# Second attention over the context replanned, self-attention masks split between two engines

## The reference, cut to what matters

```python
# cross: 16 heads of 64; query = layernorm(x), keys and values from the context
q = (einsum('btd,dhk->bthk', query, Wq) + bq) / 8
k = einsum('bsd,dhk->bshk', key, Wk) + bk
v = einsum('bsd,dhk->bshk', value, Wv) + bv
probs = softmax(einsum('bshk,bthk->bhts', k, q))
out = einsum('bthk,hkd->btd', einsum('bhts,bshk->bthk', probs, v), Wo) + bo

# self: 8 heads of 64, 5 experts, 2 chosen
wv = topk_mask(x @ Ws, 2) * sigmoid(x @ Ws)
v = einsum('bthe,btek->bhtk', wv, einsum('btd,edk->btek', x, Wv))
attn = softmax(q k^T / 8) v
out = einsum('bthe,bthk,ekd->btd', topk_mask(x @ Wd, 2), attn, Wo)
```

## Time and profile before

| | |
|---|---|
| median of 3 runs | 2669.01 us (2666.1 to 2669.58) |
| the profiled execution: time, span | 2665.16 us, 2663.4 us |
| TensorE busy, weight load | 2396.2 us (90%), 1526.1 us (57%) |
| VectorE, ScalarE, POOL busy | 1830.3 (69%), 1203.5 (45%), 857.8 us (32%) |
| mean granted clock of TensorE | 0.942 |
| first instruction of cross, of self (POOL) | 1081.82, 2160.16 us |

### The profile page before, as it was taken

How to read it: one execution, slowest core, us unless ns; L and a number is a source line. 1 busy time by engine, 2 the same in 40 slices (tenths; PEclk the granted TensorE clock), 3 DMA queues, 4 the chain that set the end, 5 groups by cost and what they waited for, 6 DMA issues and landing times. The chain is left out here.

```text
span 2663.4 us, 36143 instructions
## 1 busy us (share of the span) xinstructions
PE 2396.2 (90%) x13376; PEld 1526.1 (57%) x13376; DVE 1830.3 (69%) x3190; ACT 1203.5 (45%) x2092; POOL 857.8 (32%) x469
## 2 busy tenths in 40 slices
PE   5999999999999689799999999999999958889896
PEld 3555655655655477555565556555665545556564
DVE  6998898798788577456655665565556537867673
ACT  4555455445454200244444444444444413756485
POOL 3421221222222000175545554555455711101010
PEclk9999999999999789799999999999999977888887
DMA  3000000000000111400000000000000010000000
GB/s 110 15 1 24 17 1 25 17 1 1 17 1 1 48 40 39 117 13 1 1 24 16 1 1 25 16 1 1 1 17 1 1 59 9 1 1 24 16 1 24
DMA packets 62632, 48.62 MB, mean 18 GB/s; under 512 B 12226, under 2 KB 61954, under 8 KB 62466
## 3 DMA queue, kind: packets, MB, share of 16 engines
q1 hardware_dynamic: 62468, 46.40, 5.7%
HBM read 38.01 MB, written 8.39 MB: 17 GB/s over the span
## 5 line engine op out<-in xcount | busy, mean ns | idle before, releaser
L436 POOL TENSOR_TENSOR cross_acc_pool<-cross_acc_pool,cross_probs 128x1024 f32<-128x1024 f32 x192 | 464.4, 2419 | 163.7 <-ACT cross_probs L517 149.6
L634 DVE TENSOR_REDUCE cross_part<-cross_ring 128x1 f32<-128x512 f32 x512 | 322.7, 684 | 99.0 <-PE cross_ring L771 98.9
L422 POOL TENSOR_TENSOR latent_KR<-latent_rot 128x256 f32<-128x256 f32 x128 | 176.1, 1375 | 606.7 <-DVE latent_rot L628 606.7
L517 ACT ACTIVATE cross_probs<-cross_scores 128x1024 f32<-128x1024 f32 x256 | 256.5, 1026 | 169.4 <-PE cross_scores L803 165.8
L517 ACT ACTIVATE latent_probs<-latent_scores 128x1024 f32<-128x1024 f32 x256 | 247.7, 1020 | 86.6 <-PE latent_scores L799 86.6
L663 DVE TENSOR_TENSOR latent_acc_dve<-latent_acc_dve,latent_probs 128x1024 f32<-128x1024 f32 x192 | 258.1, 1344 | 10.0
L819 PE MATMUL cross_outT<-cross_probs,cross_VN 128*64 128x512 f32 x1024 | 250.3, 610 | 0.0
L819 PE MATMUL latent_outT<-latent_probs,latent_VN 128*64 128x512 f32 x1024 | 247.9, 605 | 0.7 <-DVE latent_probs L649 0.7
L771 PE MATMUL cross_ring<-cross_KH,cross_QH 64*128 64x512 f32 x512 | 153.3, 475 | 40.8 <-DVE cross_newt L670 23.4
L649 DVE TENSOR_SCALAR latent_probs<-latent_probs 128x1024 f32<-128x1024 f32 x256 | 167.7, 695 | 9.4 <-ACT latent_probs L517 9.3
L436 POOL TENSOR_TENSOR cross_acc_pool<-cross_probs 128x1024 f32<-128x1024 f32 x32 | 76.3, 2384 | 299.4 <-PE cross_ring L831 262.9
(11 more groups left out here) (290 smaller groups left out, 5639.0 us busy)
## 6 DMA issues: line engine op xcount, KB each, us to landing
latent_C<-in_ctx_dram SPq DMA_DIRECT2D x4, 1024.0 KB, 6.5
cross_C<-in_ctx_dram SPq DMA_DIRECT2D x4, 1024.0 KB, 6.5
latent_XN<-in_x_dram SPq DMA_DIRECT2D x4, 512.0 KB, 3.9
latent_WRAW<-in_L_xattn_Wkv_dram SPq DMA_DIRECT2D x16, 128.0 KB, 2.4
latent_X<-in_x_dram SPq DMA_DIRECT2D x4, 512.0 KB, 3.8
x_after<-latent_X SPq DMA_DIRECT2D x4, 512.0 KB, 2.9
experts_raw<-in_L_ffn_expert_w_dram SPq DMA_DIRECT2D x1, 2048.0 KB
experts_XN<-x_after SPq DMA_DIRECT2D x4, 512.0 KB, 4.0
```

The costliest lines, as they stand in the source:

```text
L422: nc.gpsimd.tensor_tensor(KR[:, 2 * t:2 * t + 2, :], rot1s[n % 2][:, :, :], rot2s[n % 2][:, :, :], ALU.add)\
L436: nc.gpsimd.tensor_tensor(acc_pool[:, :, :], first[:, :, :], probs[g % PROBS][:, :, :], ALU.add)\
L517: nc.scalar.activation(probs[g % PROBS][:, :, :], scores[g % 2][:, :, :], ACT.Exp, scale=SCALE)\
L634: nc.vector.reduce_max(part[:, qt, h, i:i + 1], bank[:, :], AX.X).then_inc(taken, 1)
```

## The change

Cross: K(s+2, 1) moves to d = 3 of step s, one step earlier than before, and K(s+2, 0) to d = 1, q(s+2) to d = 2; V stands at d = 0 and 2. `between` is empty: the maxima stand two before and two after the scores of each part. At d = 0 `behind` comes ahead of `front`. The turns of the next batch are spread one or two to a part, and K, shift and q follow them. The first output tile moves from d = 1 to d = 2. `norm` is ScalarE's correction (2 - newt) and two POOL products. The shift's operands are rounded, in cross and in self. In self, masks 1 and 3 become one VectorE product of 128x640 each.

```diff
-            for t, d in enumerate((1, 2, 3, 3)):
+            for t, d in enumerate((1, 2, 3, 3) if latent else (2, 2, 3, 3)):
                 put(late, s, d, ("out", b - 1, t))
...
         if more:
-            put(tail, s, 0, ("K", s + 1, 1))
             maxima = [("max", s + 1, qt, i, h) for i in range(KT // 4) for qt in range(QT) for h in range(2)]
-            for d, place in ((0, between), (0, mid), (1, front), (1, between), (1, mid), (2, front), (2, mid), (3, front)):
-                put(place, s, d, *maxima[:2])
-                maxima = maxima[2:]
+            for d in range(parts):
+                put(front, s, d, *maxima[4 * d:4 * d + 2])
+                put(mid, s, d, *maxima[4 * d + 2:4 * d + 4])
+        group, half = divmod(s + 2, 2)
+        if group < steps // 2:
+            if group * 2 // NP == b:
+                for i in range(2):
+                    put(tail, s, 2 * i, ("V", group, 2 * half + i))
+            elif half == 1:
+                for t in range(parts):
+                    put(tail, s, t, ("V", group, t))
+        entering = p == NP - 2 and b + 1 < B
+        if entering:
+            n = b + 1
+            put(tail, s, 0, turn(n, "c", 0, 0), ("sum", s - 1))
+            put(tail, s, 1, ("norm", s - 1), turn(n, "c", 1, 0), turn(n, "c", 0, 1))
+            put(tail, s, 2, ("K", s + 2, 0), turn(n, "c", 1, 1), turn(n, "x", 0))
+            put(tail, s, 3, turn(n, "x", 1), ("K", s + 2, 1), ("shift", s + 1), ("q", s + 2))
+            continue
         if s > 0:
             put(tail, s, 0, ("sum", s - 1))
             put(tail, s, 1, ("norm", s - 1))
...
-        elif s + 2 < steps:
-            put(tail, s, 2, ("K", s + 2, 0))
+        if s + 2 < steps:
+            put(tail, s, 1, ("K", s + 2, 0))
+            put(tail, s, 2, ("q", s + 2))
+            put(tail, s, 3, ("K", s + 2, 1))
         if more:
             put(tail, s, 3, ("shift", s + 1))
...
-            plan += front[n] + behind + scores + mid[n]
+            plan += behind + front[n] + scores + mid[n]
...
-            negtop = sb("negtop", [P, QT, 2, DH])
+            negtop = sb("negtop", [P, QT, 2, DH], f32r)
...
+                elif kind == "norm" and not latent:
+                    s = item[1]
+                    b, p = divmod(s, NP)
+                    pool.wait_ge(corrected, s + 1)
+                    nc.gpsimd.tensor_tensor(newt[:, :], newt[:, :], guess[:, :], ALU.mult).then_inc(newt_steps, 1)
+                    pool.wait_ge(newt_steps, s + 1)
+                    pool.wait_ge(evacuated, s + 1)
+                    nc.gpsimd.tensor_tensor(OT[:, p, :], OT[:, p, :], newt[:, :], ALU.mult).then_inc(normed, 1)
...
+                elif kind == "norm" and not latent:
+                    s = item[1]
+                    act.wait_ge(*freed(("sum", s)))
+                    nc.scalar.activation(newt[:, :], newt[:, :], ACT.Copy, scale=-1.0, bias=2.0).then_inc(corrected, 1)
...
                         last = nc.tensor.matmul(bank[:, qt * P:(qt + 1) * P], negtop[:, qt, :, :].rearrange("p h d -> p (h d)"),
-                                                ident[:, :], start=True, stop=True)
+                                                identr[:, :], start=True, stop=True)
...
-                elif kind == "mask":
+                elif kind == "mask" and item[2] in (0, 2):
...
+                elif kind == "mask" and item[2] in (1, 3):
+                    _, s, t = item
+                    if t == 1:
+                        dve.wait_ge(*freed(("back", s)))
+                        dve.wait_ge(scales_made, s + 1)
+                        if s >= 2:
+                            dve.wait_ge(mix_steps, mix_before[s - 1])
+                    nc.vector.tensor_tensor(masked[s % 2][:, t, :, :, :],
+                                            natural[s % 2][:, t, :, :].unsqueeze(1).broadcast_to([P, EXPERTS, 2, DH]),
+                                            scaled[s % 2][:, t, :, :].rearrange("p h e -> p e h").unsqueeze(3)
+                                            .broadcast_to([P, EXPERTS, 2, DH]), ALU.mult).then_inc(rows_gated, 1)
...
-                    dve.wait_ge(rows_masked, QT * (s + 1))
+                    dve.wait_ge(rows_masked, 2 * (s + 1))
+                    dve.wait_ge(rows_gated, 2 * (s + 1))
```

More of the change, by code:

```diff
@@ L147, in context_plan @@
             put(tail, s, 1, ("norm", s - 1))
[L148 to L160, removed]
-        elif s + 2 < steps:
-            put(tail, s, 2, ("K", s + 2, 0))
+        if s + 2 < steps:
+            put(tail, s, 1, ("K", s + 2, 0))
+            put(tail, s, 2, ("q", s + 2))
+            put(tail, s, 3, ("K", s + 2, 1))
         if more:
             put(tail, s, 3, ("shift", s + 1))
-        if s + 2 < steps:
-            put(tail, s, 3, ("q", s + 2))
     for b in range(1, B):
@@ L183, in context_plan @@
         plan += [("max", 0, qt, i, h) for i in range(KT // 4) for qt in range(QT) for h in range(2)]
-        plan += [("fold",), ("shift", 0), ("K", 1, 0), ("q", 1)] + [("V", 0, t) for t in range(KT // 2)]
+        plan += [("fold",), ("shift", 0), ("K", 1, 0), ("K", 1, 1), ("q", 1)] + [("V", 0, t) for t in range(KT // 2)]
     for n in range(steps * parts):
@@ L441, in _ @@
             nc.scalar.preload_act_table_set("natural_log_exp_and_others")
+            if not latent:
+                act.wait_ge(const_made, 1)
+                nc.scalar.activation(identr[:, :], ident[:, :], ACT.Copy).then_inc(ident_rounded, 1)
             for item in plan:
@@ L669, in _ @@
                     dve.wait_ge(guessed, s + 1)
+                    if s and not latent:
+                        dve.wait_ge(normed, s)
                     nc.vector.tensor_tensor(newt[:, :], total[:, :], guess[:, :], ALU.mult).then_inc(free[unit["sum", s] % BANKS], 1)
-                elif kind == "norm":
+                elif kind == "norm" and latent:
                     s = item[1]
@@ L991, in self_layer @@
         part, top = sb("part", [P, QT, 2]), sb("top", [P, QT, 2])
-        negtop = sb("negtop", [P, QT, 2, DH])
+        negtop, identr = sb("negtop", [P, QT, 2, DH], f32r), sb("identr", [P, P], f32r)
         scores = [ctx.enter_context(nc.psum_tensor(f"{name}_scores{i}", [P, 2, NQ], fp32)) for i in range(2)]
@@ L1006, in self_layer @@
         dve_added, pool_added = sem("dve_added"), sem("pool_added")
-        recip_made, scales_made, rows_masked = sem("recip_made"), sem("scales_made"), sem("rows_masked")
+        recip_made, scales_made = sem("recip_made"), sem("scales_made")
+        rows_masked, rows_gated = sem("rows_masked"), sem("rows_gated")
         gate_exp, gate_steps, v_steps = sem("gate_exp"), sem("gate_steps"), sem("v_steps")
-        mix_steps = sem("mix_steps")
+        mix_steps, ident_rounded = sem("mix_steps"), sem("ident_rounded")
         MADE = 7
@@ L1340, in _ @@
                     if s >= 2:
-                        dve.wait_ge(rows_masked, QT * (s - 1))
+                        dve.wait_ge(rows_masked, 2 * (s - 1))
+                        dve.wait_ge(rows_gated, 2 * (s - 1))
                     gates = rank[b % 2][:, :, HEADS + 2 * p:HEADS + 2 * p + 2, :]
@@ L1418, in _ @@
                     pe.wait_ge(max_steps, s + 1)
+                    pe.wait_ge(ident_rounded, 1)
                     for qt in range(QT):
                         last = nc.tensor.matmul(bank[:, qt * P:(qt + 1) * P], negtop[:, qt, :, :].rearrange("p h d -> p (h d)"),
-                                                ident[:, :], start=True, stop=True)
+                                                identr[:, :], start=True, stop=True)
                     last.then_inc(full, 1)
```

6 lines of the change are left out of this document (4 added, 2 removed).

## The result

The changed kernel takes 2606.41 us (median of 3 runs, 2605.82 to 2607.05) against 2669.01: 0.9768 of the time before, 95% interval 0.9746 to 0.9791. The profiled execution's span fell from 2663.4 to 2604.0. From the first POOL instruction of each stage, cross went from 1078.3 us (1081.82 to 2160.16) to 1037.1 (1082.26 to 2119.35), **-41.2**, and self, to the end of the span, from 503.2 to 484.7, **-18.6**.

A forecast was written before the change was run, and what follows sets the result against it. Cross was taken as bound by TensorE, its waits and instructions; self by three engines handing over small pieces. Cross -28.5 and self -2.6 gave -31 us, so 2638 us against 2669.01, range 2612 to 2661.

The forecast's parts named there:

- The wait behind the sum, -10: Cross: TensorE's waits for the product freeing the sum's bank shrink to 0.15 us each in 27 waits, -10 us.
- The row scaling: Cross: taking it off VectorE is worth nothing by itself, as VectorE has 10 us a step free.
- K two steps ahead: Cross: this new place of K only moves instructions about and costs nothing as long as the ring holds.
- The shift: Cross and self: rounding the shift's operands taken as 0, between bounds of +5 and -15 us.
- The rival: Cross and self: the narrow shift runs at the rounded pace, 15 us more saved, 2623 us; chance 0.28.
- The long steps, -11.7: Cross: three steps where a small VectorE product waits for POOL's add lose that wait, 3 x 3.9 = -11.7 us.
- Batch entries, turned x, first output, -8.5: Cross: shorter waits entering a batch (-2), for turned x (-2.8) and for scaled rows at the first output (-3.7).
- The end, +1.7: End of cross: row scaling by ScalarE and POOL is the longer way there, +1.7 us, bounds +1 to +4.
- Self, -2.6: Self attention: end -7, waits on ScalarE -4, mask 3 on VectorE +8.4 over some 7 steps; -2.6 us.
- VectorE becomes self's bound: Self rival: both masks lengthen all 14 steps, 26 us more than forecast, 2664 us, no change; chance 0.11.
- the shift waits for the maxima: Cross rival: negtop comes late behind POOL's adds, the shift 1.7 us late in 31 steps, 2691 us; chance 0.09.
- the waits only move: Rival: sum and batch-change waits stay; cross gives only -11.7 - 3.7 + 1.7, self -2.6: 2653 us; chance 0.14.

The follow-up runs named there:

- e2_between: Kernel before with one pair of maxima a step moved, so two score groups instead of one stand behind the sum: 2693.91 us, 1.0099.
- e9_pool: Kernel before with only the row scaling of cross moved to ScalarE and POOL: 2670.95 us, 1.0016.
- e4_rows: Changed kernel with a batch's four VectorE row products moved to part 0 of two steps, where POOL waits for the sum: 2579.67 us, 0.9671.
- e5_order: Kernel before with the new order of cross alone; row scaling on VectorE, shift plain, self untouched: 2666.45 us, 0.9994.
- e6_norm: Changed kernel with the row scaling of cross back on VectorE: 2627.59 us, 0.9848.
- e11_both: Kernel before with the new order of cross and the row scaling by ScalarE and POOL together; shift plain, self as before: 2639.49 us, 0.9892.
- e3_masks: Kernel before with masks 1 and 3 of self on VectorE; shift not rounded, cross untouched: 2659.31 us, 0.9971.
- e7_mask3: Changed kernel with mask 3 of self back on ScalarE, mask 1 staying on VectorE: 2613.32 us, 0.9803.
- e1_shift: Kernel before with rounded operands of the shift alone, in cross and in self: 2652.66 us, 0.9948.

## Why the prediction was wrong, point by point

Three terms failed: the wait behind the sum, taken at a third of its size; the rounded shift, taken at nothing; and what POOL's fuller queue and the new order do to the rows of the next batch, which has no term at all.

**The wait behind the sum, -10: mis-sized.** "I leave 0.15 us of the wait": the walk along the ring was right. The wait removed was taken at its bracket, 0.45, and not at the 1.0 us by which the starts tell it. In 31 steps that is some 30 us where I wrote 10. My own walk had it: the work ahead of the third item in the kernel before is 1.0 + 0.34 + 0.93 = 2.27 us, and the item goes 3.51 us after the sum's start, so the wait was 1.2, and one more score group fills 0.93 of it. e2_between, which leaves K(s+1, 1) directly ahead of the sum, gives back 0.7 of the 1.0; that the rest comes from K's leaving that place was not tested by itself.

**The row scaling, "by itself this is worth nothing": right by itself (e9_pool), wrong in the sum.** The claim about the whole was that K two steps ahead "cost nothing as long as the ring holds". It holds only if VectorE is free when K's low part comes, and the new place of K is behind the row scaling. So what I costed at nothing was what lets the 30 us through: with the scaling on VectorE 1.2 us a step go to the wait for K. I took the price of each part against the kernel before, and not against the kernel with the other parts in it.

**The shift, "I take 0": failed.** Cross got 13.1 us (1050.2 to 1037.1), from 0.5 us a step: ahead of AV, where the new order has it, the plain shift takes 0.98 us and the rounded one 0.48. The rival's mechanism was right, at a chance of 0.28. The row of the 256-column products beside it (0.12 each with a weight load) had the right pace; the row I took was another kind of operand. And that no narrower rounded product is in the trace was wrong. The router of the experts multiplies rounded operands of 8 columns, each with a new 128x128 weight load:

```profile
1010.40 0.25 PE L1716 MATMUL experts_routed<-experts_router_low,experts_XThigh 128*128 128x8 f32 x1
1010.51 0.25 PE L1716 MATMUL experts_routed<-experts_router_high,experts_XTlow 128*128 128x8 f32 x1
```

They stand 0.11 us apart. Between 8 columns at 0.11 and 256 at 0.12 there was little room for 0.2 at 128, so the trace spoke for the rival. From the four passes that the Trainium skill ("FP8 and Floating Point Precision", "TensorE Precision Notes") counts for true fp32 I had drawn a quarter; in the same place it is half here (0.81 to 0.40).

**The long steps, -11.7: the named wait went, a dearer one came.** Newton's product falls in POOL's idle time now (0.15 us), as I said. That "its adds end well before the sum" is true too, but I looked for the price of POOL's 2.5 us only at POOL's end. They close the gaps between its adds, and four row products of VectorE that ran in those gaps at 0.40 us now mostly wait for an add: +28 (e4_rows). This price is that of the rows' place in the kernel after, not of POOL's products alone: with the scaling on VectorE in the new order (e5_order, e6_norm) the pair in step 3 ran at 0.40, but the pair in step 4 at 2.4 and 2.6, and these steps alone cost some 21 us. So the new order had made the place of that pair a bad one, whichever engine scales. The rule that I had weighed for mask 3, of the Trainium skill ("SBUF — State Buffer", "SBUF: two separate sides"), tells this case as well, and 0.40 against 1.9 us agrees with it; I had not asked which other VectorE products it would reach.

**Batch entries, turned x, first output, -8.5:** these waits went (CTL from 7.5 to 1.6, XTL and the scaled rows to none before the stage's end), and 2.1 us for K's low part came. But these too were taken at their brackets: in e11_both the twelve steps that enter a batch are 17.3 us shorter beyond the gain of a quiet step. Which of the moved items gave how much, no run separates. **The end, +1.7:** TensorE's last two long waits of the stage are 7.8 and 5.5 where before they were 4.8 and 3.6, +4.9, above my upper bound of +4.

**Self, -2.6: mis-sized, and one interplay missed.** The end gave 8.6 (7 forecast). The p = 2 steps gave 10.0 by the masks alone (e3_masks) and 13.0 with the shift, where I had -4 for the waits: in e3_masks 1.6 shown microseconds fewer made a step 3.0 shorter (37.25 to 34.28). That the clock, 0.80 in this stage, makes a wait cost what follows it too is argued here, not shown. Mask 3 pays the add as forecast. The nine other steps lost 11.2 with both masks and the plain shift, where I had +8.4 for mask 3; with the rounded shift they lost 3.7, and taking mask 3 away (e7_mask3) gives back 2.7 of that. **Open:** why the shift's 10.9 us of TensorE time saved in e1_shift shorten self by 0.4 alone and by 11 together with the masks. Longer waits for the sum's reciprocal (6.7 to 10.6 us) take 3.9 of it in e1_shift, but in the kernel after they are as long (11.7); the rest I did not find.

**The other rivals.** "VectorE becomes self's bound" and "the shift waits for the maxima" did not happen: TensorE waited 2.2 us for it in 960. That the waits only move came true for the order alone, and not for the whole.

Summed, in cross: order and POOL's scaling -28.2 (of it +28 for the rows), shift -13.1. In self: masks -7.5, shift with them -11.

By steps, the -28.2 is made of 31 quiet gains of 1.08 (-33.5), the batch entries beyond that (-17.3), the steps 3, 4, 11, 12, 19 and 20 (+14.5: Newton's wait gone, the rows' waits come), the last step with the end of the stage (+3.9), and the rest (+4.3).

## What to carry over

Price a wait by the distance between starts, less what the instructions cost elsewhere, and look what the clock does behind it; the bracket was too low at each place looked at here. When an edit takes away a wait, cost every other part again in the kernel without it: parts that are worth nothing alone can be worth all of it together. An engine made busier is to be asked not only when it ends, but who used its gaps.

## What the runs showed of the hardware

A 128x512 product of two tensors on POOL takes 1.28 us, a little more than half of its 128x1024 add (2.38). Rounding its operands halves the 128-column product, and a VectorE product that writes rounded values is no slower for it (negtop in self 0.43 in both kernels). One wait of 3.3 us was followed by 5.4 us at a granted clock of 0.56.
